# Input layouts, the first loads on SP, and who sets the rows of ones

## What is computed

```
x = x + tanh(g_xattn) * attention(layernorm(x), ctx, ctx, Wq, bq, Wk, bk, Wv, bv, Wo, bo)
x = x + tanh(g_ffn)   * ffn(layernorm(x), clip_x, clip_down, w_gate, w_up, w_down)

attention(query, key, value, ...):      # x and ctx are 8 x 512 x 256, 16 heads of 16
    q, k, v = projections, split into heads
    q = q * cos + rotate_half(q) * sin   # k likewise
    out = softmax(q k^T * 16 ** -0.5) v
    return out @ Wo.T + bo

ffn(x, ...):                            # inner width 704, everything fake-quantised to 8 bits
    h = quant(silu(xq @ w_gate.T) * (xq @ w_up.T))
    return h @ w_down.T
```

## Time and profile before

| | us |
|---|---|
| median of three timed runs | 595.54 |
| the profiled execution | 595.78 |
| its span, first to last instruction | 594.0 |
| stage A, up to the first instruction of stage B on DVE | 107.4 |
| stage B | 107.4 to 503.4 |
| stage C | 503.4 to 594.0 |

### The profile page before, as it was taken

The page is one execution under the profiler, slowest core; times in us unless marked ns, Lnnn a source line. Parts: engine busy times, 40 slices in busy tenths (PEclk is TensorE's granted clock), DMA queues, the critical chain, the costliest instruction groups (busy, mean ns, idle before and its releaser), DMA issues. The chain is left out here.

```text
span 594.0 us, 18538 instructions
## 1 busy us (share of the span) xinstructions
PE 562.3 (95%) x6586; PEld 262.2 (44%) x6586; DVE 532.6 (90%) x688; ACT 444.7 (75%) x873; POOL 248.8 (42%) x370
## 2 busy tenths in 40 slices
PE   7989999999999999999999999999999999988985
PEld 3555655233344444444444444444444433433363
DVE  3799998999999999999899899899899885799988
ACT  2766767357787897897897897797798662888694
POOL 8699999701310336453224214215215211465400
PEclk9999999999999999999999999999999999999999
DMA  8759877553422343332332243245231000000035
GB/s 283 248 167 301 243 198 201 145 122 76 83 61 66 80 74 56 72 87 54 66 88 60 57 88 70 54 77 83 54 70 41 2 1 1 2 1 1 0 107 178
DMA packets 61255, 55.21 MB, mean 93 GB/s; under 512 B 11040, under 2 KB 58784, under 8 KB 61216
## 3 DMA queue, kind: packets, MB, share of 16 engines
q1 hardware_dynamic: 61216, 54.70, 36.8%
HBM read 37.62 MB, written 16.78 MB: 92 GB/s over the span
## 5 line engine op out<-in xcount | busy, mean ns | idle before, releaser
L922 ACT ACTIVATE prob<-st_ps 128x512 f32<-128x512 f32 x512 | 280.4, 597 | 62.5 <-PE st_ps L780 55.2
L780 PE MATMUL st_ps<-q,k 98*32 98x512 bf16 x2048 | 178.4, 380 | 2.9 <-ACT prob L922 1.9
L982 DVE TENSOR_REDUCE negm<-xT_ps 128x2 f32<-128x1024 f32 x128 | 154.4, 1206 | 7.9 <-PE xT_ps L338 7.4
L982 DVE TENSOR_REDUCE negm<-v_ps 128x2 f32<-128x1024 f32 x128 | 154.2, 1205 | 3.8 <-PE v_ps L338 3.8
L804 PE MATMUL pv_ps<-prob,v_u 128*32 128x512 f32 x1024 | 132.5, 592 | 0.6 <-ACT prob L922 0.3
L780 PEld LDWEIGHTS st_ps<-q,k 98*32 98x32 bf16 x2048 | 57.1, 95 | 92.3 <-ACT prob L922 34.2
L1174 POOL TENSOR_TENSOR msplit<-negm,onesf 128x16 bf16<-128x16 f32 x32 | 7.1, 222 | 206.7 <-DVE negm L982 206.7
L338 PE MATMUL xT_ps<-k,q 96*32 96x512 bf16 x1024 | 78.5, 379 | 1.1 <-DVE negm L982 1.0
L338 PE MATMUL v_ps<-k,q 96*32 96x512 bf16 x1024 | 78.0, 380 | 1.0 <-DVE negm L982 0.6
L338 PEld LDWEIGHTS xT_ps<-k,q 96*32 96x32 bf16 x1024 | 27.1, 96 | 36.2 <-issue 13.0
L804 PEld LDWEIGHTS pv_ps<-prob,v_u 128*32 128x32 f32 x1024 | 31.1, 110 | 26.9 <-issue 2.6
(11 more groups left out here) (155 smaller groups left out, 784.6 us busy)
## 6 DMA issues: line engine op xcount, KB each, us to landing
qk_parts<-parts SPq DMA_DIRECT2D x96, 128.0 KB, 2.6
k<-qk_parts SPq DMA_DIRECT2D x192, 64.0 KB, 2.8
q<-qk_parts SPq DMA_DIRECT2D x192, 64.0 KB, 2.9
ctx<-in_ctxT SPq DMA_DIRECT2D x8, 512.0 KB, 4.6
X<-in_x SPq DMA_DIRECT2D x8, 512.0 KB, 8.3
out<-X SPq DMA_DIRECT2D x7, 512.0 KB, 3.0
q<-mrow SPq DMA_DIRECT2D x64, 4.0 KB, 2.1
wf<-in_w_down SPq DMA_DIRECT2D x1, 704.0 KB, 4.7
```

Source lines behind the costliest of these rows:

```text
L780: last = nc.tensor.matmul(score_bank(i)[lo:lo + COLS, :], k6[g][:, h, kt * P + lo:kt * P + lo + COLS], q6[g][:, h, :], start=True, stop=True)
L922: nc.scalar.activation(prob[kt % 2][:, h, :], score_bank(HPU * kt + h)[:], ACT.Exp, scale=SCALE).then_inc(exp_done, 1)
L982: nc.vector.tensor_reduce(negm[g % 2][:, lo:lo + 2], pair[:], op=ALU.max, axis=AX.X, negate=True).then_inc(mx_read, 1)
```

## The change

It has five parts.

1. The host lays x, ctx and the three projection weights out so that each partition's share of one load is one run: 4 KB for x and ctx, 2 KB for the weights. The output tensor becomes 128 x 32 x 256, so that a send of four tiles writes runs of 4 KB.
2. SP issues `wk`, ctx 0, x 0 and `wv`, and waits until ctx 0 has landed. Then it issues the biases, `cs` and `wq`, waits until x 0 has landed, and issues x 1, ctx 1, x 2, the gates, x 3 and x 4.
3. x 5, x 6 and x 7 are issued in `body(1)`, `body(2)` and `body(3)`, right behind the store of index 3.
4. Each batch of x has a semaphore of its own, and the statistics of a batch wait for that batch alone.
5. DVE sets the rows of ones, in front of its first statistics, and POOL no longer does. DVE's first rope waits for these memsets.

```
+        x_in = [sem(f"x_in{b}") for b in range(B)]
+        k_ones = sem("k_ones")
...
-                    sp.dma_start(X[:, tiles, :], x_v[:, tiles, :]).then_inc(arrived, DMA)
+                def load_x(b):
+                    sp.dma_start(X[:, TPB * b:TPB * (b + 1), :], a["x"][b]).then_inc(x_in[b], DMA)
...
-                    sp.dma_start(ctx[b % 2][:], ctx_v[:, :, b * S:(b + 1) * S]).then_inc(ctx_in[b % 2], DMA)
+                    sp.dma_start(ctx[b % 2][:], a["ctxT"][b]).then_inc(ctx_in[b % 2], DMA)
...
                     store(sp, b - 1, 3)
+                    if b + 4 < B:
+                        load_x(b + 4)
                     if b > 1:
                         load_late(4 * (b - 2), 4 * (b - 1))
...
-                        if b < 3:
-                            dve.wait_ge((x0_in, x1_in, x2_in)[b], DMA)
-                        else:
-                            dve.wait_ge(x_in, DMA * (B - 3))
+                        dve.wait_ge(x_in[b], DMA)
...
+                for g in range(UPB):
+                    nc.vector.memset(k6[g][ROWS:ROWS + MROWS, :, :], 1.0).then_inc(k_ones, 1)
                 statistics(0, range(TPB))
                 x_moments(0)
+                dve.wait_ge(k_ones, UPB)
...
-                for g in range(UPB):
-                    last = nc.gpsimd.memset(k6[g][ROWS:ROWS + MROWS, :, :], 1.0)
-                last.then_inc(const_ready, 1)
...
+def by_partition(w, tiles):
+
+    w = np.asarray(w)
+    return w.reshape(-1, tiles, P, w.shape[-1]).swapaxes(1, 2)
...
-    out = nc.dram_tensor("out", (B * S, D), F32, kind="ExternalOutput").ap()
+    out = nc.dram_tensor("out", (P, NT, D), F32, kind="ExternalOutput").ap()
```

More of the change, by code:

```diff
@@ L391, in body @@
                         load_unit(sp, 0, UNITS[b][0], (UNITS[b][1],))
-                sp.dma_start(wk[:], a["wkT"].rearrange("(c p) n -> p c n", p=P)).then_inc(k_in, DMA)
+                sp.dma_start(wk[:], a["wkT"]).then_inc(k_in, DMA)
                 load_ctx(0)
-                load_x(0, x0_in)
+                load_x(0)
+                sp.dma_start(wv[:], a["wvT"]).then_inc(v_in, DMA)
+                sp.wait_ge(ctx_in[0], DMA)
                 sp.dma_start(bias[:], a["bkq"]).then_inc(bias_in, DMA)
                 sp.dma_start(cs[:], a["rope"]).then_inc(bias_in, DMA)
-                sp.dma_start(wv[:], a["wvT"].rearrange("(c p) n -> p c n", p=P)).then_inc(v_in, DMA)
-                sp.dma_start(wq[:], a["wqT"].rearrange("(c p) n -> p c n", p=P)).then_inc(q_in, DMA)
-                load_x(1, x1_in)
+                sp.dma_start(wq[:], a["wqT"]).then_inc(q_in, DMA)
+                sp.wait_ge(x_in[0], DMA)
+                load_x(1)
+                load_ctx(1)
+                load_x(2)
                 sp.dma_start(gates[:], a["gates"].partition_broadcast(P)).then_inc(gate_in, DMA)
[L402 to L405, removed]
+                load_x(3)
+                load_x(4)
                 load_ctx(2)
@@ L620, in _ @@
                 pool.wait_ge(const_ready, CONSTS)
-                for g in range(UPB):
-                    last = nc.gpsimd.memset(k6[g][ROWS:ROWS + MROWS, :, :], 1.0)
-                last.then_inc(const_ready, 1)
                 pool.wait_ge(ln_const_ready, len(LN_CONST))
-                pool.wait_ge(const_ready, CONSTS + 1)
                 scale_and_shift(0)
@@ L1644, in _ @@
             def _(sp):
-                out_v = out_dram.rearrange("(t p) d -> p t d", p=P)
+                out_v = out_dram
                 def send(t0, t1, ready):
@@ L1683 @@
     flat = {
-        "x": np.asarray(x).reshape(B * S, D), "ctxT": np.asarray(ctx_1024).reshape(B * S, D).T,
+        "x": by_partition(x, TPB), "ctxT": by_partition(np.asarray(ctx_1024).reshape(B, S, D).swapaxes(1, 2), KC),
         "gates": np.concatenate([np.asarray(v) for v in (g_xattn, g_ffn, L0_ffn_clip_x, L0_ffn_clip_down)]),
-        "wqT": halves(L0_xattn_Wq).T, "wkT": halves(L0_xattn_Wk).T, "wvT": np.asarray(L0_xattn_Wv).T,
+        "wqT": by_partition(halves(L0_xattn_Wq).T, KC)[0], "wkT": by_partition(halves(L0_xattn_Wk).T, KC)[0], "wvT": by_partition(np.asarray(L0_xattn_Wv).T, KC)[0],
         "woT": paired(np.asarray(L0_xattn_Wo).T), "bkq": np.concatenate([halves(L0_xattn_bk), halves(L0_xattn_bq)]).reshape(4, P).T,
@@ L1697 @@
     scratch = nc.dram_tensor("qk_parts", (3, 4, P, B * S), BF16, kind="Internal").ap()
-    out = nc.dram_tensor("out", (B * S, D), F32, kind="ExternalOutput").ap()
+    out = nc.dram_tensor("out", (P, NT, D), F32, kind="ExternalOutput").ap()
     build(nc, aps, scratch, out)
     r = run_bass_kernel_spmd(nc, [arrays], core_ids=[0])
-    return r.results[0]["out"].reshape(B, S, D)
+    return r.results[0]["out"].swapaxes(0, 1).reshape(B, S, D)
```

## The result

| | before | after |
|---|---|---|
| median of ten timed runs (us) | 595.92 | 599.37 |
| their range | 595.06 to 598.16 | 597.71 to 601.82 |
| the profiled execution | 595.78 | 598.94 |
| its span | 594.0 | 597.1 |

The ratio after to before is 1.0054, with a 95% interval of 1.0038 to 1.0071. The change makes the kernel slower, by 3.4 us between the medians and by 2.3 to 4.2 by the interval. The forecast was 595.7 and its range ended at 597.2. The time came out near rival D.

The account below looks back on a forecast made before the run. In stage A, DVE, PE and POOL were taken to set the time in turn, SP's queue near its end. 0.32 + 0 - 1.17 + 1.05 = +0.20 on 595.78 gave 595.98, as a median 595.7; range 593.3 to 597.2.

Parts of the forecast that it names:

- rival D: TensorE's clock falls to 1.2 GHz idling after early v; q matmuls double, 3 or so on the path, 598.7; chance 0.07.
- First loads held apart, 0: SP's two waits among stage A's first loads: earlier x 0 hidden by memsets, early v needed by nobody; 0 us.
- Rows of ones, +0.32: Four memsets on DVE before the first statistics take 8.8 us, so statistics start at 9.5 instead of 9.18.
- Rival B: Memsets on DVE are cheap, 2.5 us in all; x 0 sets the start, -2.2, 593.3; chance 0.13.
- `cs`: Load behind SP's first wait, needed by the k rope at 11.2: lands by 9 to 13.3; 0 taken, up to 0.6.
- x batch by batch, -1.17: Stage A, DVE: statistics of batch 3 no longer wait for batches 4 to 7, saving 1.17 us on the path.
- x 5 to 7 within the batches, +1.05: SP's queue in stage A: x 6 delays stores 0.39, x 7 0.66, reaching ACT at 80.44; x 5 is free.
- Rival A: SP's queue has slack and absorbs the issues of x 6 and x 7: -0.85, 594.7; chance 0.20.
- Rival C: x 6 and x 7 load full DMA engines; the store at 76.28 lands 1.5 later, +1.7, 597.2; chance 0.11.
- Long runs, 0: New layouts for loads and output: neither SP's issue time nor the transfer rate gains; 0, with 0.1 to 0.3 either way.

Follow-up runs that it names:

- the last kernel: The changed kernel with all memsets of ones on POOL and x 5 to 7 issued at the beginning; 593.45 us against 595.42 before, ratio 0.9969.
- the second trace of before: The kernel before, unchanged, profiled once more; that execution took 594.54 us.
- early x: The changed kernel with x 5, 6 and 7 issued at the beginning, behind x 4; 596.36 us against 596.13 before, ratio 1.0005.
- early v: The kernel before with the load of `wv` issued right behind x 0; 595.97 us against 595.86 before, ratio 0.9997.
- late v: The changed kernel with `wv` issued behind SP's second wait; 597.36 us against 595.86 before, ratio 1.0028.
- the first experiment: The changed kernel with 14 filler matmuls on TensorE between v and the transposes of batch 0; 596.61 us against 596.13 before, ratio 1.0015.
- late x on the layouts: The kernel before with the new layouts, a semaphore per batch and x 5 to 7 within the batches; 595.36 us against 595.86 before, ratio 0.9988.

## Why the prediction was wrong

*The step that failed* is "First loads held apart, 0", and in it the sentence "Nothing waits for v ... : 0". It is true that nothing waits for v. But v had kept PE busy until just before the transposes, and without it there PE stood still for 3.53 and came back at 1.2 GHz. The forecast thus took the clock's grant as fixed, a term that the sum doesn't have. This is rival D. It was priced at 3 and given 0.07, and it measured 2.15 at the q rope (2.0 by the fillers). The argument against it was the idling of 1.87 before v, which had not cost the grant. That is a row on a gap half as long as the one that came, and the working itself had PE idle from 13.0 to 16.9 but for the transposes. I should have read the new idle stretch as a state that no row had yet shown. Its chance should have been far above 0.07. The gap was also longer than the working had it, 3.53 and not some 2.5, because k took 3.70 and v was over at 11.9 and not at 13.0. Even so, D alone isn't the whole miss of 3.1 at stage B: 0.75 more come from x 5 to 7 and 0.24 from the semaphores' term.

*Rows of ones, +0.32*: measured +0.27. DVE began at 1.23, not 0.74, and each memset took 1.76 with 0.38 of idling behind it, 2.14 in all, where 2.2 was taken from the upper bound. The Trainium skill's page "VectorE: DVE Perf Modes", section "Zero memsets can be issued as uint32 (trn2)", led to an estimate of 2.13 each and 8.5 for four. The trace has 1.76 for one, less than the estimate, 2.14 from start to start, which agrees with it, and 8.18 from the first start to the last end. Rival B falls. But as a price in this kernel, 0.27 hides what counts: the memsets stood in front of data that was there at 7.05. All four on POOL instead bring the q rope to 18.64.

*`cs`*: bounded by 9 and 13.3 for its landing. In after it landed 5.3 behind its issue at 5.09, so at 10.4, and in the last kernel at 11.0. It costs 0 behind the memsets, as taken.

*x batch by batch, -1.17*: the wait is gone, and the step between the q rope and the k rope is -0.93, since one operation between them (L285) took 1.01 where it had taken 0.68. The number is right, but what it was put down to isn't shown. The wait is 0.15 with the layouts and the single semaphore, and 0.41 in the second trace of before. And the statistics of batch 3, which had waited until 24.22, start at 25.38 in after, so with the loads in their old order the late q of batch 0 alone would have covered it. What the semaphores are needed for is part 3: with one for all, batch 3 would wait for x 7.

*x 5 to 7 within the batches, +1.05*: the right direction and a partly wrong path. In after it is 1.80 and in the mean of the traces 1.24. The slack of 0.27 in front of the stores of x 6's batch was read rightly: they start 0.28 later. What wasn't in the sum is that these stores then issue and land more slowly, with x 6 and four weights in front of them, by 1.4 together. x 7 took 0.64 of SP, as priced, but behind the place where the step begins. The prediction looked for ACT's longer wait at 80.44, where it stayed at 1.98; it grew at 55.53, from 1.79 to 3.47. Rival A (the slack hides it) falls. Rival C had the slower landing, but behind x 7, and put it at 1.5; here 0.9 to 1.0 of it come in behind x 6. The split into parts is read from one pair of traces. The direction holds over all: ACT's wait at the first place is 2.2 to 4.6 in the seven traces with late x and at most 2.7 in the nine with early x, at the next one, behind x 7, the means are 2.8 and 2.3, and near 80 us late x makes no difference.

*Long runs, 0*: right inside this change only, because the memsets cover it; wrong as a statement on the layouts. The bound (0.08 for 512 KB) rested on 348 and 367 GB/s, in stretches where most transfers still had the short runs. With the new layouts alone the rate is 416 to 422, and the loads that stand in front of one another add the gain up. The Trainium skill's page "DMA: Bandwidth & Descriptors", section "Specifications", gives 512 bytes as the least transfer for line rate, by which longer runs should gain nothing. The measurement differs: going from 1 and 2 KB to 4 KB, with the weights from 1 to 2 KB, brings x 0 in 2.1 us earlier and makes a ratio of 0.9967. So here the measurement decides against the rule.

The sum with measured terms: 0.27 + 2.15 - 0.93 + 1.80 = +3.29 at stage B; the span has +3.1.

What stays open. Which gap brings the clock down isn't settled by its length: in stage A 2.28, 2.42 (early x) and 3.53 did, but 1.87, 1.98 (early v, at 36.8 us) and 2.13 (late v, at 61.3 us) did not, while in stage B 1.85 to 2.06 did and 1.40 and 1.62 did not. The amount of work ahead of the gap differs between these, and no run varied it alone. SP's two waits were not tried alone. Also open is why the interval with late x scatters from 80.45 to 82.1, what makes the runs with early x 2.9 us faster than after, and where the launches with a lower mean clock lose it, since only one execution of a set has a trace. The mean clock itself is a rough sign: in the last kernel it is 0.998, and its trace shows the clock low only from 588 us on, when PE has done its last matmul.

## What to carry to other kernels

When a transfer is moved ahead so that its consumer runs earlier, look at the hole that is left where it ran. Here a hole of 2.4 to 3.6 us on PE halved the clock for what came next, and that next was the work everyone waited for. A cheap filler tells whether it is so. Work "hidden" on another engine should be held against when its data comes with the whole change in place: four memsets that cost 0.27 by the old arrival of x 0 (9.18) cost 2.4 by the new one (7.05), and moved to POOL they are what the first batch waits for.

## What the runs showed of the hardware

- The granted clock fell to 1.2 GHz behind waits of 1.85 to 3.57 us, and stayed there for 3 to 7 us although PE was busy again: after, 14 to past 20 us; `mrow` in stage B, 133 to 136 us. Other waits, up to 2.13 us, left it at 2.4 GHz.
- The same k matmuls of batch 0 took from 3.70 (after) over 4.42 to 6.09 us (late x on the layouts). The matmuls of the later batches took 3.6 in each, so I read this as a clock that comes up at another time in each launch. The eight fillers ahead of them fit this: they took 3.23 (after) to 3.60 us, 0.40 to 0.45 each, where the 14 fillers of the first experiment took 0.23 each. It is a reading: the windows list 1.00 for this stretch in all of them.
- Runs of 4 KB instead of 1 KB make x 0 land 5.4 after its issue instead of 7.4 (layouts alone; 512 KB, with other loads in the queue), and the rate of the first loads rises from 347 to 381 GB/s to 416 to 422. The whole kernel needs 53,831 packets instead of 61,255 for the same 55.21 MB.
- A DVE memset of 2048 bfloat16 on 2 partitions took 1.76 us, the same as on POOL, and left 0.38 before the next.
